# Two graph layers on an 8192-node graph: the first layer's weights applied once, ahead of the neighbour sum, and row-block segments that begin one block earlier

## The reference

```
deg  = clip(sum(adj, 1) + 1, 1)
z    = concat([x, (adj @ x + x) / deg]) @ W0 + b0          # W0: 128 x 64
h    = relu(z);  h = h / max(norm(h), 1e-12)
x1   = layernorm(x + h)
n1   = (adj @ x1) / (sum(adj, 1) + 1)
out  = layernorm(x1 + concat([x1, n1]) @ W1.T)             # W1: 64 x 128
```

## Time and profile before

| | |
|---|---|
| median of 3 runs | 790.53 us (790.47 to 792.68) |
| the profiled execution | 794.09 us |
| its span | 792.3 us |
| mean granted clock of TensorE | 0.946 of full speed |
| PE, DVE, ACT, POOL busy | 697.7, 709.1, 621.0, 201.7 us |
| HBM read, written | 270.6 MB, 2.1 MB |

### The profile page before, as it was taken

One profiled execution on the slowest core, in us unless ns is written; L12 is line 12 of the kernel. 1 busy time (PEld: TensorE's weight loads), 2 busy tenths in 40 slices (PEclk: granted clock), 3 DMA queues, 4 the chain that ended last, 5 costly groups with the idle time before them and its releaser, 6 DMA issues.

```text
span 792.3 us, 28217 instructions
## 1 busy us (share of the span) xinstructions
PE 697.7 (88%) x11285; PEld 638.3 (81%) x11285; DVE 709.1 (90%) x2687; ACT 621.0 (78%) x848; POOL 201.7 (25%) x302
## 2 busy tenths in 40 slices
PE   1477868888898889999999999999999999999992
PEld 0467757777787778888889989899999989889992
DVE  4699977989999999999999999989999989878894
ACT  4798887989898989898988889787878889740037
POOL 2262513535413133334222030201102020201024
PEclk9988896989999999999999999999999999999997
DMA  9999999999999999999999999999999999800004
GB/s 304 388 419 419 419 419 401 408 420 410 421 417 416 415 416 395 421 393 421 390 417 385 404 381 393 372 344 384 345 411 361 404 350 368 314 2 2 2 15 96
DMA packets 46121, 274.56 MB, mean 347 GB/s; under 512 B 12642, under 2 KB 12706, under 8 KB 13218
## 3 DMA queue, kind: packets, MB, share of 16 engines
q1 hardware_dynamic: 45184, 270.55, 86.3%
q0 software_dynamic: 576, 2.10, 0.7%
q10 hardware_dynamic: 226, 0.07, 0.0%
HBM read 270.60 MB, written 2.10 MB: 344 GB/s over the span
## 4 chain that ended last, share of the span: by engine, by line
PE 48%; DVE 29%; issue 8%; DMA 6%; POOL 5%; ACT 3%; ACTq 0%; DVEq 0%; POOLq 0%; SPq 0%
PE s_ps L360 22%; DVE e L737 10%; PE u_ps L378 7%; DVE t_sb L744 6%; PE p_ps L346 6%; DMA a_in<-in_adj 3%; POOL small L1088 3%; PE z_ps L396 3%; DMA xl<-in_x 3%; PE z_ps L393 3%; PE z_ps L417 2%; DVE u_sb L744 2%; PE u_ps L428 1%; PE p_ps L428 1%; DVE a_in L744 1%
## 5 line engine op out<-in xcount | busy, mean ns | idle before, releaser
L542 ACT ACTIVATE junk<-a_in 128x2048 uint8<-128x2048 uint16 x256 | 489.2, 1918 | 4.0 <-DMA a_in<-in_adj 4.0
L360 PE MATMUL s_ps<-xh,t_sb 128*128 128x129 f16 x4096 | 386.7, 250 | 18.6 <-DVE t_sb L744 15.5
L360 PEld LDWEIGHTS s_ps<-xh,t_sb 128*128 128x128 fp8e4 x4096 | 311.3, 102 | 48.4 <-DVE t_sb L744 19.4
L737 DVE TENSOR_SCALAR e<-a_in 128x2048 fp8e4<-128x2048 f32 x256 | 310.2, 1222 | 8.2 <-DMA a_in<-in_adj 7.7
L1096 POOL COPY store<-pk 128x32 uint32<-128x32 uint32 (+1 forms) x250 | 119.8, 521 | 313.2 <-ACT pk L551 313.2
L346 PE MATMUL p_ps<-pow_bf,e 128*128 128x16 bf16 x4096 | 142.5, 170 | 51.7 <-DVE e L737 48.8
L346 PEld LDWEIGHTS p_ps<-pow_bf,e 128*128 128x128 fp8e4 x4096 | 128.6, 97 | 68.8 <-DVE e L737 62.7
L744 DVE TENSOR_SCALAR t_sb<-pk 128x128 uint32<-128x128 uint32 x1024 | 150.8, 219 | 6.5 <-ACT pk L551 6.0
L1088 POOL TENSOR_TENSOR small<-small,minus_half 128x4 f32<-128x4 f32 x32 | 65.3, 2040 | 228.0 <-DVE small L798 176.4
L378 PE MATMUL u_ps<-xh,u_sb 128*128 128x128 f16 x1488 | 99.1, 218 | 0.0
L378 PEld LDWEIGHTS u_ps<-xh,u_sb 128*128 128x128 fp8e4 x1488 | 88.9, 97 | 1.2
(11 more groups left out here) (102 smaller groups left out, 512.6 us busy)
## 6 DMA issues: line engine op xcount, KB each, us to landing
a_in<-in_adj SPq DMA_DIRECT2D x256, 1024.0 KB, 8.9
xl<-in_x POOLq DMA_DIRECT2D x4, 512.0 KB, 15.8
out_h<-e SPq DMA_DIRECT2D x8, 256.0 KB, 2.6
w_sb<-in_L_gnn_W ACTq DMA_DIRECT2D x1, 32.0 KB
w_raw<-in_L_gnn_W ACTq DMA_DIRECT2D x1, 32.0 KB
b_sb<-in_L_gnn_b ACTq DMA_DIRECT2D x1, 0.2 KB
```

What stands on the lines that cost most here:

```text
L360: last = nc.tensor.matmul(s_ps[:, n % 2, at:GW], t_sb[:, b, :], xh[:, b, at:GW], start=(b == 0), stop=False)
L542: nc.scalar.activation(junk[:, t % 2, :], halves[t % R], ACT.Copy, scale=1.0 / 128, accum_out=half_sum[:, n, c:c + 1]).then_inc(s_half, 1)
L737: nc.vector.tensor_scalar(e8[:, c, :], a_in[:, t % R, :], 1.0, None, ALU.is_equal, saturate=False).then_inc(s_e, 1)
```

## The change

1. **Weights ahead of the sum.** (adj @ x) @ W = adj @ (x @ W). In row block 1 the kernel now computes, for all 16 groups of four node blocks, acc = x @ W0[0:64] + b0 (fp32, kept) and y = x @ W0[64:128] times 2^11, split into fp16 halves `y_hi`, `y_lo`, which take the place of x's halves in the features (`yg`). A group takes four transposes of x (PE, L392), a copy (ACT, L602), four fp32 matmuls with `wy_sb` of 65 rows and 128 columns (PE, L401), a copy of the high half (ACT, L607), a copy to `acc` and a subtraction (DVE, L722, L723). The groups are laid one ahead of each other, four to each quarter of row block 1. `split_x` in row block 0 is gone.
2. **Batches.** The neighbour sum is now already in z's space: `layer1` (DVE) divides it by the degree, adds `acc` and takes the max with 0. `transpose_cat`, `take_cat`, `dense`, `take_z` and DVE's wait for them are gone.
3. **Order in a batch.** `layer1` and `norm` at k = 1; `residual` and `normalise` at k = 2; `transpose_h` after the last pack of k = 2; `dense_h` at the head of k = 3; `take_g` behind chunk 0 of k = 3, `low_part` and `begin_acc` behind DVE's compare of chunk 1.
4. **Segments.** `START` is 11, 19 .. 51 and `LAG` 3, so `low(q)` stays 8, 16 .. 48. The wait of PE for the batch's low half moves from the head of the row block to the quarter that reads it first.
5. `weights` moves from row block 1 to 2, the guard over squares from 2..5 to 3..6 (and looks at y), three more small loads of weights, and PE and DVE wait for all six of them at the start. The tail's order is drawn together in the same way.

```diff
-START = [0, 12, 20, 28, 36, 44, 52]
-LAG = 4
+START = [0, 11, 19, 27, 35, 43, 51]
+LAG = 3
...
-            def transpose_cat(e):
...
+            def transpose_x(g):
+                pe.wait_ge(s_x[g * NC // NE], 16)
+                if g >= 2:
+                    pe.wait_ge(s_xt, g - 1)
+                for k in range(BR):
+                    last = nc.tensor.transpose(xt_ps[g % 2][0:F, k, :], x_sb[:, g * BR + k, :], ident[:, :])
+                last.then_inc(s_xtps, 1)
+            def dense_x(g):
+                pe.wait_ge(s_xt, g + 1)
+                if g >= 2:
+                    pe.wait_ge(s_ylo, g - 1)
+                for k in range(BR):
+                    last = nc.tensor.matmul(y_ps[g % 2][:, k, :], x_t[:, g % 2, k, :], wy_sb[:, :],
+                                            start=True, stop=True)
+                last.then_inc(s_yps, 1)
...
-            def dense(e):
...
-                if e >= 0 and k == 2:
-                    dense(e)
+                if e >= 0 and k == 3:
+                    dense_h(e)
                 for c in range(NC):
                     pack_chunk(n, c)
-                    if e >= 0 and (k, c) == (1, 3):
-                        transpose_cat(e)
-                    if n == START[seg(n)] and n and c == 0:
+                    if n == 1:
+                        for g in range(c * NE // NC, (c + 1) * NE // NC):
+                            if g == 0:
+                                transpose_x(0)
+                            if g + 1 < NE:
+                                transpose_x(g + 1)
+                            dense_x(g)
+                    if e >= 0 and (k, c) == (2, 3):
+                        transpose_h(e)
+                    begins, last_b = n and n == START[seg(n)], low(seg(n)) - 1
+                    if begins and c < 2 and c == last_b // CB:
                         pe.wait_ge(s_glo, low(seg(n)) // BR)
                     if n:
                         sum_quarter(n - 1, c)
...
+            def take_xt(g):
+                act.wait_ge(s_xtps, g + 1)
...
+                nc.scalar.copy(x_t[0:F, g % 2, :, :], xt_ps[g % 2][0:F, :, :]).then_inc(s_xt, 1)
+            def take_y(g):
+                act.wait_ge(s_yps, g + 1)
+                nc.scalar.copy(y_hi[:, g * BR:(g + 1) * BR, :], y_ps[g % 2][:, :, F:2 * F]).then_inc(s_yhi, 1)
...
                 sum_codes(n, 0)
-                if e >= 0 and k == 2:
-                    take_z(e)
-                if n == 0:
-                    split_x(0)
+                if n == 1:
+                    take_xs(0)
+                if e >= 0 and k == 3:
+                    take_g(e)
...
+            def split_y(c):
+                for g in range(c * NE // NC, (c + 1) * NE // NC):
+                    rows = slice(g * BR, (g + 1) * BR)
+                    dve.wait_ge(s_yhi, g + 1)
+                    nc.vector.tensor_copy(acc[:, rows, :], y_ps[g % 2][:, :, 0:F])
+                    nc.vector.tensor_tensor(y_lo[:, rows, :], y_ps[g % 2][:, :, F:2 * F], y_hi[:, rows, :],
+                                            ALU.subtract).then_inc(s_ylo, 1)
...
-            def mean(e):
+            def layer1(e):
...
-                nc.vector.tensor_tensor(acc[:, rows, :], s_sb[:, :, :], bc(small[:, 0, :], BR),
-                                        ALU.mult).then_inc(s_mean, 1)
+                for k in range(BR):
+                    ins = nc.vector.scalar_tensor_tensor(out=z_sb[:, k, :], in0=s_sb[:, k, :],
+                                                         scalar=small[:, 0, k:k + 1], in1=acc[:, e * BR + k, :],
+                                                         op0=ALU.mult, op1=ALU.add)
+                link(ins)
+                link(nc.vector.tensor_scalar(r_sb[:, :, :], z_sb[:, :, :], 0.0, None, ALU.max))
```

More of the change, by code:

```diff
@@ L694, in _, with guard_y @@
             nc.vector.tensor_copy(pow_bf[:, :], pow_f[:, :]).then_inc(s_pow, 1)
[L695 to L709 removed]
+            link(nc.vector.memset(yg[:, :, 2 * HP:GW], YS))
+            link(nc.vector.memset(wy_sb[F:F + 1, F:2 * F], 0.0))
+            link(nc.vector.memset(x_t[F:F + 1, :, :, :], 1.0))
+            dve.wait_ge(s_w, 96)
+            nc.vector.tensor_scalar(wy_sb[0:F, F:2 * F], wy_sb[0:F, F:2 * F], YS, None, ALU.mult).then_inc(s_wy, 1)
+            def split_y(c):
+                for g in range(c * NE // NC, (c + 1) * NE // NC):
+                    rows = slice(g * BR, (g + 1) * BR)
[3 more added lines that the diff above has]
+                                            ALU.subtract).then_inc(s_ylo, 1)
+            def guard_y(q):
+                cols = slice(q * CB, (q + 1) * CB)
+                link(nc.vector.tensor_tensor(scratch, y_hi[:, cols, :], y_hi[:, cols, :], ALU.mult))
+                link(nc.vector.tensor_reduce(ysq[:, cols], scratch, AX_X, ALU.add))
             def centre_w(w, rows, one):
@@ L894, in verdict @@
                 link(nc.vector.tensor_reduce(bad[:, 2:3], sums, AX_X, ALU.max))
-                link(nc.vector.tensor_scalar(sums, xsq[:, :], XSQ_MAX, None, ALU.is_gt))
-                link(nc.vector.tensor_scalar(want, xsq[:, :], XSQ_MIN, None, ALU.is_lt))
+                link(nc.vector.tensor_scalar(sums, ysq[:, :], YSQ_MAX, None, ALU.is_gt))
+                link(nc.vector.tensor_scalar(want, ysq[:, :], YSQ_MIN, None, ALU.is_lt))
                 link(nc.vector.tensor_tensor(sums, sums, want, ALU.max))
@@ L1122, in _ @@
                 if e >= 0 and k == 2:
-                    root(0, e)
+                    root(1, e)
                 if n:
                     keep(n - 1)
-                if e >= 0 and k == 2:
-                    root(1, e)
+                if e >= 0 and k == 1:
+                    root(0, e)
             keep(NB - 1)
```

210 lines of the change are left out of this document (91 added, 119 removed).

## The result

The changed kernel takes 819.38 us (median of 4 runs, 812.7 to 823.74). Of the kernel before there are, beside it, the three runs of the prediction (790.47 to 792.68) and one of 1243.4 us, which lifts its median to 791.61 us and is left out of the ratio: 1.0348, 95% interval 1.0248 to 1.0449. The direction was forecast (slower, 798 us), the size was not. The profiled execution took 822.23 us, its span is 820.0 us, 27.7 more than before.

The account below looks back on a forecast made before the run. Bound taken: the stream for the first 200 us, DVE right behind it up to 371 us, PE for the rest. 23.5 us of lost stream less 15.3 of gains, about + 8 on the 790.53 median, gave 798 us; range 783 to 812.

Parts of the forecast that it names:

- I take half, 11: X stage in row block 1: half of the 22 us that 1.2 GHz throughout would add; stage ends at 72.5 us.
- the schedule: Hand schedule of the x stage at full clock: start 25.5, quarters 22.8, between quarters 13.1; end at 61.4 us.
- cold from end to end: Rival: x stage at low clock throughout, 36 us of stream lost, 811 us; chance 0.15.
- Loss = end of stage - 49: Stream time lost to the x stage, reckoned from chunk 14's arrival before and after; 23.5 us at half clock.
- Late batches: Batches from 371 to 700 us: DVE's two waits go, less DVE's added work; 7.6 us gained.
- middle: Four batches from 206 to 371 us: 1.8 us of wait goes, DVE's added work comes; 1.6 us lost.
- early dips: Clock dips at 100 to 200 us, where a cold dense block holds ACT and costs the stream; 1.5 us gained.
- the end of the stream: From DVE's last compare to PE's last row-block sum: 12.2 us become 7.9, less 1.5 for DVE's accumulator start; 2.8 us gained.
- The tail: Tail: dense matmuls, their clock dip and the transposes leave PE's run of sums; 5 us gained, 3 if DVE is full.
- The segments: New START and LAG: nothing gained, 0 to at most 4 us lost by PE's waits at row blocks 11 and 19.
- Fast stage: Rival: fp32 work keeps PE at 2.4 GHz in the x stage, 12.4 us of stream lost, 787 us; chance 0.25.
- Caught up: Rival: stream slack before 200 us lets ACT run ahead and win back the lost stream, 777 us; chance 0.05.

Follow-up runs that it names:

- run 5: The changed kernel with 60 idle fp8 products on PE ahead of row block 1's first pack; 808.44 us, ratio 1.0248.
- run 4: The changed kernel with DVE's weights and two of four guards inside the x stage, the other guards in row blocks 7 and 8; 811.26 us.
- run 1: The changed kernel without PE's transposes and matmuls of the x stage (x split in place of x @ W, output not the first layer's); 782.45 us.
- 6: The changed kernel with 60 idle fp8 products ahead of row block 1's first pack and 8 behind every group of the stage; 810.19 us.
- run 12: The changed kernel with only DVE's order altered: next compare and unpack ahead of the quarter's takes in row block 1; 809.02 us, ratio 1.0235.
- run 9: The changed kernel with the x stage dealt out, two groups beside each of the eight chunks of row blocks 0 and 1; 822.76 us.
- run 2: The changed kernel with segments as before the change (START from 12, LAG 4); 818.83 us, ratio 1.0334.
- run 14: The changed kernel, groups dealt out beside chunks 3 to 7, node blocks paired, compares ahead, DVE's jobs among groups, 60 idle products; 800.33 us.

## Why the prediction was wrong in size

**The step that failed, first: "I take half, 11".** The mechanism was right: the stage holds ACT and DVE, six buffers fill, the stream stands, no later slack takes it back. So was the schedule: between quarters 4.8, 3.4 and 4.9 us were forecast, and the change has 4.5, 3.4 and 4.5; 61.4 us was forecast for the stage's end at full clock, and run 5, cold in its last quarter only, ended at 65.6. But in the change PE was at 1.2 GHz for all sixteen groups. I had argued from the earlier trace rows, where PE came to full speed some 6 us after it got steady work. That was a sum of fp8 by fp16; here fp32 transposes and products for 54 us, with breaks of 1.3 to 2.3 us, did not bring the clock up in this run. The stage ended at 80.9 us, not 72.5: 8.4 us. Why the clock stayed down here and came up in run 4, whose first quarter is the same, is open. The rival "cold from end to end" was the case, with its 811 us nearest to the result; it had the cold group too dear (1.53 x 1.9 = 2.9 us for 2.56) and so the end at 85.4.

**The second: "Loss = end of stage - 49".** By it 80.9 gives 31.9 us; run 1 against the change makes it 38.4. Nearly all of the missing 6.5 was lost by 85 us, when the stream had stood for 37.3, so it is not a slow stream behind the stage; from 85 to 100 us that brings 394 GB/s. The 49 comes from chunk 14, which ACT takes at 54.5 us in the kernel before. By then the stream there has brought 20 MB (25 us at 306 GB/s, 29.5 at 417), which is x and 17 chunks: two more than the 15 that the formula counts are on their way (a load takes 8.9 us in the median from issue to landing, and one lands every 2.5). When the stream stands, these run dry as well. At 86.4 us (end + 5.5), where the formula has chunk 14 there, the change has brought 17.6 MB, 2.3 MB less than the kernel before at 54.5, and that is the 5.6 us beyond 31.9. Four more runs with the stage in row block 1 agree: in runs 4, 5, 6 and 12 the stage ended at 66.6, 65.6, 68.6 and 65.9, and the stream stood 5.9, 7.1, 7.3 and 6.4 us longer than the formula gives (6.3 in the change).

**A term without an entry: DVE's one-time jobs behind the stage.** DVE, with 12.8 of 40 us busy in the stage, gets `weights` and four guards, 13 us, right behind it, and never stops from 84 to 146 us. The diff shows the move of these jobs by one row block; the prediction has no term for what they stand beside. It is a small one: some 3 us by the rows of run 4, and the jobs begin at 88.7 us, when the 37.3 are already lost.

**What was in the schedule but not seen as a cost.** I took the 3.4 to 4.9 us between quarters as given. A compare that waited for nothing stood there behind a wait for PE. In this form of the stage that is 2 us (run 12); where the groups are dealt out it is 2.3 to 2.4 us at each of six chunks (run 9), and moving the groups without the order made the kernel no faster (822.76 us).

**The gains were right in kind and 4.6 us too high.** Forecast were 15.3; run 1, without PE's part of the stage, is 10.7 shorter than the kernel before. Late batches, middle, early dips and the end of the stream were forecast at 10.3 us together: run 1 has 8.3 (from 2.1 behind at the first sum to 6.2 ahead at the last). The tail was forecast at 5, and is 4.5 in run 1 and in the change. The 2.1 us by which the first sum comes late were not forecast; their cause is open. From 560 to 620 us PE and DVE are now equally busy (57.4 and 57.2 of 60 us). DVE's two waits are all but gone, and a new one of 6.4 us for the catch-up matmuls came, which I had not named. The segments are worth nothing that can be told, as said (run 2).

**The other rivals.** "Fast stage" (787 us, a loss of 12.4): in run 5, at full clock for three quarters of four, the stream stood 23.7 us, and even run 14, mostly at full clock and with shorter groups, lost 18.1. "Caught up": excluded by the table.

So 798 became 819: 8.4 from the clock, 6.5 from the formula, 4.6 from the gains, and 1.1 because the two profiled spans lie 27.7 us apart and the medians (790.53 and 819.38) 28.9; the rest is rounding. The account is that of the profiled execution, which took 822.23 us; what the clock did in the other three (812.7 to 823.74) no trace shows.

## What to carry to other kernels

Work that is done once, ahead of a stream that already runs at its ceiling, costs what it stops the stream for, and no later relief gives that back. Count that in bytes against the stream as it was, not from the arrival of one chunk: what is on its way runs dry too (5.6 us here). Write down every engine's order there as well: an operation whose data is ready belongs ahead of the one that waits for another engine, above all before work is dealt out in more pieces, and one-time jobs belong into the waits, not behind them (3 us here). The clock of a stage that starts from an idle TensorE is a range, not a mean: carry both ends through the sum. And where a version comes out faster, look at the clock in its trace before crediting the edit: in run 12 it was 2 us of order and 13 of clock.
